# Shared-expert and attention pass: attention steps one half pair later, transposed rows in two banks, another order of four small matmuls

## The reference

```python
xn = _layernorm(x, axis=-1)
x = x + attention(xn) + ffn(xn)
# attention: scores = q k^T / sqrt(16), -10000 outside the window; softmax + 1e-9; ctx = attn v; ctx @ Wo.T + bo
# ffn: combined = sum over the 2 chosen experts of c_e * down_e(silu(gate_e xn) * up_e xn)
#      shared_out = down_s(silu(gate_s xn) * up_s xn)
```

## Time and profile before

| what | us |
|---|---|
| median of three runs (2117.62, 2126.46, 2126.1) | 2126.1 |
| the profiled execution, its own time | 2116.85 |
| its span | 2115.1 |
| PE busy in the span | 1737.2 (82%) |
| DVE busy | 1251.5 (59%) |
| ACT busy | 882.7 (42%) |
| POOL busy | 774.1 (37%) |
| mean granted clock of PE, share of 2.4 GHz | 0.907 |

### The profile page before, as it was taken

One profiled execution on the slowest core, in us unless ns is written; L12 is line 12 of the kernel. 1 busy time (PEld: TensorE's weight loads), 2 busy tenths in 40 slices (PEclk: granted clock), 3 DMA queues, 4 the chain that ended last, 5 costly groups with the idle time before them and its releaser, 6 DMA issues.

```text
span 2115.1 us, 40817 instructions
## 1 busy us (share of the span) xinstructions
PE 1737.2 (82%) x12377; PEld 1482.9 (70%) x12378; DVE 1251.5 (59%) x3737; ACT 882.7 (42%) x1721; POOL 774.1 (37%) x725
## 2 busy tenths in 40 slices
PE   6936455544999999999999888888888888888887
PEld 6925454443888888888888667666666677666666
DVE  6653232322666666666666657766766667776762
ACT  2211111112454545555555345544554554555552
POOL 0014423320000000000000057777777777777775
PEclk9998777676999999999999869999999998999998
DMA  8347767665444444444444456767777777777752
GB/s 281 131 148 231 221 211 225 213 211 187 149 152 150 152 150 150 150 148 154 149 151 150 103 139 161 166 154 166 165 165 161 164 171 166 166 165 165 165 144 81
DMA packets 262429, 350.61 MB, mean 166 GB/s; under 512 B 26736, under 2 KB 172400, under 8 KB 260336
## 3 DMA queue, kind: packets, MB, share of 16 engines
q1 hardware_dynamic: 210304, 278.21, 47.4%
q0 software_dynamic: 12288, 33.57, 6.2%
q10 hardware_dynamic: 39792, 38.28, 5.5%
HBM read 219.43 MB, written 129.50 MB: 165 GB/s over the span
## 4 chain that ended last, share of the span: by engine, by line
PE 57%; issue 12%; SPq 11%; DVE 9%; DMA 6%; ACT 4%; POOL 1%; DVEq 0%; ACTq 0%; POOLq 0%
PE psum L149 31%; PE psum L784 10%; SPq L577 9%; PE psum L1263 6%; PE psum L1227 4%; DVE plain_arena L1430 4%; DMA plain_arena<-xn_d 3%; PE psum L1249 2%; PE psum L855 2%; DVE split_arena L1440 1%; ACT plain_arena L1357 1%; PE psum L1276 1%; DVE plain_arena L1449 1%; ACT plain_arena L1363 1%; SPq L580 1%
## 5 line engine op out<-in xcount | busy, mean ns | idle before, releaser
L149 PE MATMUL psum<-split_arena 128*128 128x256 f32 (+1 forms) x5328 | 994.1, 343 | 32.2 <-DVE plain_arena L1453 13.8
L149 PEld LDWEIGHTS psum<-split_arena 128*128 128x128 f32 x5328 | 840.7, 200 | 146.5 <-DVE plain_arena L1453 24.3
L1430 DVE CUSTOM_DVE_ANT_0 plain_arena<-psum,mask 128x256 f32<-128x256 f32 (+1 forms) x1024 | 337.5, 384 | 235.1 <-PE psum L1227 218.7
L1357 ACT ACTIVATE plain_arena<-psum 128x512 f32<-128x512 f32 (+1 forms) x512 | 252.3, 546 | 409.1 <-PE psum L1249 388.1
L1212 POOL MEMSET split_arena<- 128x256 f32 x1 | 0.3, 311 | 699.0 <-ACTq L138 699.0
L784 PE MATMUL psum<-split_arena 128*128 128x256 f32 x1872 | 233.8, 285 | 0.0
L784 PEld LDWEIGHTS psum<-split_arena 128*128 128x128 f32 x1872 | 226.9, 192 | 0.1
L1227 PE MATMUL psum<-split_arena 48*128 48x256 f32 (+1 forms) x1024 | 177.2, 359 | 35.8 <-DVE plain_arena L1430 24.8
L614 POOL DMA_INDIRECT sorted_d<-plain_arena,q_idx x128 | 124.1, 970 | 199.5 <-DVE q_idx L701 163.8
L1159 POOL TENSOR_SCALAR_AFFINE_SELECT plain_arena<-plain_arena 128x1024 f32<-128x1024 f32 x128 | 140.0, 1094 | 148.6 <-ACT plain_arena L1357 146.4
L901 ACT ACTIVATE plain_arena<-psum 128x512 f32<-128x512 f32 x156 | 93.3, 598 | 220.0 <-PE psum L149 219.8
(11 more groups left out here) (132 smaller groups left out, 2030.0 us busy)
## 6 DMA issues: line engine op xcount, KB each, us to landing
plain_arena<-in_gate_w SPq DMA_DIRECT2D x39, 512.0 KB, 5.0
plain_arena<-in_up_w SPq DMA_DIRECT2D x39, 512.0 KB, 6.1
plain_arena<-in_down_w SPq DMA_DIRECT2D x39, 512.0 KB, 6.9
plain_arena<-sorted_d SPq DMA_DIRECT2D x39, 512.0 KB, 3.8
y_d<-plain_arena ACTq DMA_DIRECT2D x39, 512.0 KB, 3.6
plain_arena<-in_x SPq DMA_DIRECT2D x32, 512.0 KB, 3.9
plain_arena<-xn_d SPq DMA_DIRECT2D x32, 512.0 KB
q_d<-split_arena SPq DMA_DIRECT2D x64, 256.0 KB
```

The source lines that it names most:

```text
L149: last = pe.matmul(out, lhs_t(p), rhs(q), start=(begins and c == 0 and k == 0), stop=(ends and c == len(chunks) - 1 and k == 2), skip_grou ...
L1357: act.activation(b_pt[:, g % 2, 2 * p + par, 4 * half:4 * half + n, :].rearrange("p k s -> p (k s)"), psum[:, 2 + par, 0:n * P], ACT.Exp, ...
L1430: last = dve.tensor_tensor_reduce(b_junk[:, 2 * par + i % 2, 0:cols], psum[:, par, at:at + cols], mask[:, 2 * P - cols:2 * P], -1.0, 3e38, ...
```

## The change

All lags of the attention steps behind the maxima grow by one slot; what is tied to fixed slots doesn't move with them, so the two meet in other slots. `turn_rows` goes from slots 5 and 6 to 3 and 4 (its ACT and DVE steps to 4 and 5), and its second chunk goes into bank 4, between the sums of groups 1 and 2 of the batch before. The waits follow: `turn_maxima` of group 0 waits for the first chunk's `rows_lo`, `values` of group 2 for the second one's, the second chunk for `copy_sums` of group 1. In `scores_t` the four matmuls go par 0, par 1, par 0, par 1, with one wait for both exponentials ahead of all. `load_qk` goes from slots 3, 7, 11, 15 to 4, 8, 12 and 0 of the next turn.

```diff
-        LAG_TM, LAG_M, LAG_T, LAG_SEL, LAG_V, LAG_U = 4, 5, 7, 9, 13, 14
-        LAG_US, LAG_UL, LAG_RC, LAG_SP, LAG_N, LAG_CH, LAG_CL = 15, 16, 18, 19, 21, 22, 23
+        LAG_TM, LAG_M, LAG_T, LAG_SEL, LAG_V, LAG_U = 5, 6, 8, 10, 14, 15
+        LAG_US, LAG_UL, LAG_RC, LAG_SP, LAG_N, LAG_CH, LAG_CL = 16, 17, 19, 20, 22, 23, 24
...
-                    b, g = due_group(t, h, 6)
+                    b, g = due_group(t, h, 7)
                     if b is not None:
                         load_v(b, g)
-                    if h in (3, 7) and valid(t):
-                        load_qk(sp, t, 2 + h // 7)
-                    if h in (11, 15) and valid(t + 1):
-                        load_qk(sp, t + 1, h // 15)
+                    if h in (0, 4, 8) and valid(t) and not (h == 0 and is_first(t)):
+                        load_qk(sp, t, 1 + h // 4)
+                    if h == 12 and valid(t + 1):
+                        load_qk(sp, t + 1, 0)
...
-                if g == 1:
-                    after(pe, b_xlo, 2 * b)
+                if g == 0:
+                    after(pe, b_xlo, 2 * b - 1)
...
-                for par in range(2):
-                    rows = slice(64 * par, 64 * par + 50)
-                    after(pe, b_ex, 32 * b + 2 * r + par - 1)
-                    for j in (2 * half, 2 * half + 1):
+                after(pe, b_ex, 32 * b + 2 * r)
+                for j in (2 * half, 2 * half + 1):
+                    for par in range(2):
+                        rows = slice(64 * par, 64 * par + 50)
...
+                if g == 2:
+                    pe.wait_ge(b_xlo, 2 * b + 2)
...
-                    pe.wait_ge(b_nc, 4 * (b + 1) + (1 if valid(b + 1) else 0))
+                    pe.wait_ge(b_nc, 4 * b + 4)
                 else:
-                    pe.wait_ge(b_xlo, 2 * b + 1)
+                    pe.wait_ge(b_ue, 4 * b + 2)
                 for a in range(T):
-                    last = pe.transpose(psum[:, 5, a * P:(a + 1) * P],
+                    last = pe.transpose(psum[:, 5 - c, a * P:(a + 1) * P],
...
-                    if h in (5, 6) and valid(t - 1):
-                        turn_rows(t - 1, h - 5)
+                    if h in (3, 4) and valid(t - 1):
+                        turn_rows(t - 1, h - 3)
...
-                    if h in (6, 7) and valid(t - 1):
-                        rows_hi(t - 1, h - 6)
+                    if h in (4, 5) and valid(t - 1):
+                        rows_hi(t - 1, h - 4)
...
-                    if h in (6, 7) and valid(t - 1):
-                        rows_lo(t - 1, h - 6)
+                    if h in (4, 5) and valid(t - 1):
+                        rows_lo(t - 1, h - 4)
```

More of the change, by code:

```diff
@@ L1252, in scores_t @@
                                          start=True, stop=True)
-                    last.then_inc(b_t, 1)
+                        if j % 2 == 1:
+                            last.then_inc(b_t, 1)
             def values(b, g):
@@ L1381, in rows_hi @@
                 act.wait_ge(b_tr, 2 * b + c + 1)
-                act.copy(b_xt[:, 0, c, :], psum[:, 5, :]).then_inc(b_xhi, 1)
+                act.copy(b_xt[:, 0, c, :], psum[:, 5 - c, :]).then_inc(b_xhi, 1)
             def scale_routed(b, k):
@@ L1468, in rows_lo @@
                 dve.wait_ge(b_xhi, 2 * b + c + 1)
-                dve.tensor_tensor(b_xt[:, 1, c, :], psum[:, 5, :],
+                dve.tensor_tensor(b_xt[:, 1, c, :], psum[:, 5 - c, :],
                                   b_xt[:, 0, c, :].bitcast(F32), ALU.subtract).then_inc(b_xlo, 1)
```

## The result

| kernel | median us | runs | lowest to highest |
|---|---|---|---|
| before | 2122.14 | 20 | 2107.45 to 2132.76 |
| after | 2143.97 | 20 | 2116.94 to 2173.64 |

The changed kernel is slower, by about 1%: ratio 1.0063, 95% interval 1.0036 to 1.0089; the medians of all runs give 1.0103 (2143.97/2122.14), since the ratio leaves out runs over 1.5% above a kernel's fastest, nine of the changed kernel's twenty. The forecast was 2062 us, range 2010 to 2107; 2144 lies outside it. The profiled execution of the changed kernel has a span of 2144.4 us against 2115.1.

What follows compares the result with a forecast made beforehand. PE's own work was taken to bound slots 8 to 15, a PE-ACT-DVE-PE round trip slots 3 to 7, DVE slots 0 to 2. Terms -15, -63, +21 and -3 gave -60, 2057, plus 5: 2062 us, range 2010 to 2107.

Steps and rivals of the forecast that it cites:

- three releasers: PE's attention-phase waits before: `turn_rows` behind `rows_lo` 43.0 us, `turn_maxima` behind the split 33.2, `scores` behind the maxima 21.9.
- Stretch B: Slots 3 to 7 of a turn, rows in two banks: 19.6 to 15.4 us, -4.2 a turn, bounds -5.1 and -2.0.
- The 0.5 us for `finish`: Slot 8: `gate_up_half` 0 waits for `finish`, behind the reciprocal in DVE's slot 7; 0 to 1.2 us, taken as 0.5.
- Stretch A: Slots 0 to 2 of a turn, set by DVE: 11.7 to 10.6 us, -1.1 a turn, bounds -2.8 and +0.5.
- Order of the four matmuls: Transposed step in `scores_t`: pairs already overlap, so 0; bounds 0 and -36 us over 256 steps.
- rival 3: The matmul order counts: three quarters of 36 us, -27 on the forecast, 2035 us; chance 0.08.
- stretch C: Slots 8 to 15 of a turn, steps landing together on ACT: +1.5 us a turn, bounds -0.5 and +2.6.
- a blocked context lo in full: DVE's context lo, moved to slot 12 ahead of slot 13's maxima: counted within the upper bound of +2.6 us a turn.
- DMA queue: SP's loads of q and k behind the reciprocal's store: cost 0 without slack; 0 to 2 us in two places a turn.
- rival 5: q and k land late, each place costing wait and lower clock, 5.4 us against 3.8: +19, 2141 us; chance 0.08.
- the sign of failure as a whole: The forecast fails as a whole if PE's clock drops at a new place in slots 3 to 15.
- The end: PE's last wait, 7.8 us for the last chunk's `hidden_lo`: now ahead of `normalise`, which comes about 2 us later; -3 us.

Runs made afterwards that it cites:

- the first experiment: The changed kernel with the loads of q and k back in slots 3, 7, 11 and 15, ahead of the reciprocals' spread: 2285.7 us, ratio 1.0792.

## Why the prediction was wrong

- **Where the idle time lay**: three releasers were said to hold nearly all of PE's idle time. They hold 98.1 of the 130 us that the view lists.
- **Stretch B** was right in kind and near in size: 15.4 us forecast, 14.6 on average; its new wait in slot 6 was costed at 0.4, and the trace shows 4.1 us over 8 times, 0.3 a turn. The banks alone confirm it (14.5). The clock over slots 6 and 7 was 1.00, as the sign of being right asked. The 0.5 us for `finish` was put into B, though slot 8 opens C; without it the forecast of B was 14.9.
- **Stretch A**: 10.6 forecast, 11.1 measured, and the split in slot 15 takes 0.17 us for each half, as expected. But `scores` still waits in slot 1 (1.54 at 1747.26), so only 0.3 us a turn came of it. The turn that I took as the pattern, at 11.7 us, was longer than the mean of 11.4.
- **Order of the four matmuls**: 0 forecast, 0 measured. The rule of the Trainium skill ("TensorE: Matmul & The Clock Gate", "Part 3: Packing small matmuls — row/col tiling"), that weights load under a running matmul only in another row group, stood beside rival 3. The order that should give one more such overlap gains no time here: ratio 0.9995.
- **The step that failed is stretch C**, forecast at +1.5 us a turn with a bound of +2.6; measured +6.3, and +14.3 in the first experiment. Three terms were wrong, two of them booked outside C. What the +1.5 was taken for, the steps moved onto ACT's slot 11, is not seen: `gate_up_half` waits for `hidden` (L1456) only 0.4 us in slots 12 and 13 in all. With k early and the gather in the row it does wait there, 11.9 us over 22 times.
- First, the bound of +2.6 less the 1.3 us of the two moved steps leaves 1.3 us for "a blocked context lo in full". In the kernel before it takes up to 1.6 us, 0.74 when free. There it meets POOL just ahead of a gather; moved one slot, it meets a row of seven operations. One slot for this operation alone costs 2.6% in the old kernel. I had read the Trainium skill's remark ("GPSIMD Engine Reference", "8. Key points") that GpSimd and VectorE contend when VectorE has two SBUF inputs, and applied it to the split only, which got 2 us shorter in slot 15; I didn't ask of each moved DVE operation what POOL does in its new slot. The traces agree: context lo has two SBUF inputs and took up to 7.5 us here, 8.4 in the first experiment.
- Second, "DMA queue: cost 0, but with no slack". The wait is there, nearly all in slot 12: 30.6 us over 15 times, 2.0 us a turn, and 1.4 us in slot 4. The bound of "0 to 2 us" held it, the 0 did not. In one turn the reciprocal ended at 1718.16, the eighth load was issued at 1725.76, and `scores` went on at 1731.37: 13.2 us, where I had 10.6 to 11.6. About half is the way to the last issue, 7.6 us where it was 6.2; the load of v stands between the reciprocal's store and its spread, as before, and the spread follows it later. The other half is the landing (L814: median 5.2, maximum 8.7 us; 4.3 and 5.9 before, over the same stretch). Why it lands later is not shown. The timeline of SP:

```profile
1718.27 0.51 SPq L1115 DMA_DIRECT2D rz_d<-plain_arena  x1
1719.14 0.60 SPq L1099 DMA_DIRECT2D plain_arena<-v_d  x1
1720.77 0.61 SPq L1119 DMA_DIRECT2D plain_arena<-rz_d  x1
1721.64 0.33 SPq L812 DMA_DIRECT2D split_arena<-q_d  x1
...
1725.76 0.37 SPq L814 DMA_DIRECT2D split_arena<-k_d  x1
```

- Third, the wait for `finish` in slot 8 was taken as 0.5 us and is 1.95. Ahead of `finish` stand a split that POOL's zeroing, now in even slots, blocks, and the reciprocal; the reciprocal back in its slot took only 0.5 us a turn of it away (timeline of DVE):

```profile
1771.75 0.60 DVE L1443 CAST split_arena<-plain_arena 128x16 fp32r<-128x16 f32 x1
1772.38 1.01 DVE L1445 TENSOR_TENSOR split_arena<-plain_arena,split_arena 128x16 fp32r<-128x16 f32 x1
1773.31 0.54 DVE L1462 RECIPROCAL plain_arena<-plain_arena 64x64 f32<-64x64 f32 x1
1773.78 0.62 DVE L1479 TENSOR_TENSOR plain_arena<-psum,plain_arena 128x512 f32<-128x512 f32 x1
```

  The zeroing that left slot 15 came to meet the splits of slots 7 and 3: the two halves take 1.6 us after slot 7 where they took 0.35, and mostly 1.3 to 1.9 after slot 3 where they mostly took 1.1. What the one split gained, the others lost.
- **The rivals**: rival 5 gave 2141 for late loads, close to what came, and its sign (PE waiting for `k_d`) and the sign of failure as a whole (a lower clock at a new place in C, 0.82 and 0.74) both came. Its mechanism is real, but the near number is luck: it named slots 4 and 12, and the waits are nearly all in slot 12; it had no wait for `finish` of this size and no long context lo; and taking the late loads away made the time longer, not shorter. A chance of 0.08 for it was too low for a step that I had myself found without slack.
- **The end**: PE's last wait for `hidden_lo` fell from 7.8 to 3.4 us, -4.4 where -3 was forecast.

Not settled: the wide spread of the changed kernel's runs (2117 to 2174 us) would fit a number of long turns that differs between executions, but I have profiles of one execution only. Which boundaries between two POOL operations let DVE in is open too. The split's first half got in between L1172 and L1193 and, at 1771.75 above, between L1159 and L1161. The context's lo did not get in at the same kind of boundary inside the row of seven, nor did the split's first half in the 3.7 us with the banks alone. Why some turns escape where the context's lo alone was moved was not tried.

## What to carry to other kernels

When steps move between slots, go through every VectorE operation on SBUF and ask what GpSimd runs in the new slot and how long its row is until it next waits or issues a DMA; price it at the whole row, not at one operation. A DMA issue placed between GpSimd's operations was such a break here. It has a price only where something waits for that DMA: moved by two slots, two gathers made slot 0 longer by 1.1 us; moved by one slot, one gather left it at 2.3. And when a step has no slack, try the change's parts alone: here one part (the banks) is worth -1.8% and the other hides that.

## What the hardware showed that I had not expected

- A VectorE operation with two SBUF inputs waited for a whole row of seven GpSimd operations, 7.4 to 8.4 us where it takes 0.74 alone; cut in four, the first part waited 8.0 us and the next three 0.3 each. One gather issued within the row brought it down from 8.4 to 1.4 us in slot 12 of every full turn.

- Removing waits of 31.9 us made the kernel 142 us slower, since with k late GpSimd itself waited within its row, up to 2.7 us, and VectorE got in there; with the gather in the row as well it was 20 us slower (2164.29 less 2143.97).
